# Two attention layers on one core: q and k kept in float32 in row tiles of 32, with the other TensorE jobs placed between the maxima

## The reference, cut to what matters

```python
q = split_heads(x @ Wq + bq)      # 16 heads of 16; x here is the layer-normalised x
k = split_heads(x @ Wk + bk)
v = split_heads(x @ Wv + bv)
attn = einsum('bhqd,bhkd->bhqk', q, k) / sqrt(16)
attn = attn + slopes[:, None, None] * (arange(T) - (T - 1))    # layer 0 only
attn = where(causal, attn, finfo.min)
o = einsum('bhqk,bhkd->bhqd', softmax(attn), v)
x = x + o @ Wo + bo
x = x + ffn(layernorm(x))         # layer 0: int weights, hidden 704; layer 1: fp8 weights, hidden 768
```

## Time and profile before

| | us |
|---|---|
| median of 3 runs | 438.63 |
| lowest, highest | 436.79, 441.16 |
| profiled execution, span | 441.7 |
| TensorE busy | 410.0 |
| VectorE busy | 297.1 |
| ScalarE busy | 232.9 |
| GpSimd busy | 170.2 |

### The profile page before, as it was taken

How to read it: one execution, slowest core, us unless ns; L and a number is a source line. 1 busy time by engine, 2 the same in 40 slices (tenths; PEclk the granted TensorE clock), 3 DMA queues, 4 the chain that set the end, 5 groups by cost and what they waited for, 6 DMA issues and landing times.

```text
span 441.7 us, 14528 instructions
## 1 busy us (share of the span) xinstructions
PE 410.0 (93%) x6328; PEld 237.2 (54%) x6328; DVE 297.1 (67%) x596; ACT 232.9 (53%) x377; POOL 170.2 (39%) x250
## 2 busy tenths in 40 slices
PE   5799789999999988999999998998999999888997
PEld 5356564555555347544377466544555553465476
DVE  4636489999998216521336586899999981188883
ACT  3535355577776973221101541655877769635950
POOL 4107013314033144478692000234361544453770
PEclk9989799999999999999999997999999999999999
DMA  6899550000000000200100479400000000000002
GB/s 204 129 239 263 128 148 4 4 3 4 4 2 5 4 1 6 65 8 9 64 0 0 120 200 224 106 5 4 3 4 3 4 5 2 2 1 0 1 26 71
DMA packets 21657, 22.97 MB, mean 52 GB/s; under 512 B 2588, under 2 KB 20858, under 8 KB 21594
## 3 DMA queue, kind: packets, MB, share of 16 engines
q1 hardware_dynamic: 20498, 19.03, 17.8%
q0 software_dynamic: 544, 2.49, 1.9%
q10 hardware_dynamic: 552, 0.53, 0.4%
HBM read 8.27 MB, written 1.05 MB: 21 GB/s over the span
## 4 chain that ended last, share of the span: by engine, by line
PE 71%; DVE 14%; ACT 4%; DMA 3%; issue 3%; POOL 2%; SPq 2%; ACTq 0%; DVEq 0%
PE ps L785 11%; PE ps L765 11%; DVE mx L1258 11%; PE ps L743 10%; PE ps L916 8%; PE ps L1012 5%; PE ps L944 4%; PE ps L921 4%; ACT prob L1141 4%; PE ps L677 4%; PE ps L980 4%; DMA col_rows<-in_L_ffn_up_scale 3%; PE ps L845 3%; PE ps L751 2%; POOL xn L605 1%
## 5 line engine op out<-in xcount | busy, mean ns | idle before, releaser
L1258 DVE TENSOR_REDUCE mx<-ps 128x1 f32<-128x512 f32 (+3 forms) x304 | 181.1, 654 | 28.9 <-PE ps L751 24.1
L1141 ACT ACTIVATE prob<-ps 128x1024 f32<-128x1024 f32 (+1 forms) x192 | 145.4, 812 | 63.4 <-PE ps L765 63.1
L743 PE MATMUL ps<-kS,qS 96*32 96x512 bf16 (+21 forms) x1536 | 111.9, 321 | 4.4 <-DVE mx L1258 3.0
L590 POOL TENSOR_SCALAR_AFFINE_SELECT prob<-prob 128x256 f32<-128x256 f32 x128 | 51.9, 412 | 163.9 <-ACT prob L1141 162.5
L765 PE MATMUL ps<-qS,kS 101*32 101x512 bf16 (+7 forms) x1536 | 95.2, 326 | 3.7 <-ACT prob L1141 3.6
L785 PE MATMUL ps<-prob,v 128*32 128x512 f32 (+3 forms) x768 | 80.1, 489 | 0.6 <-POOL prob L590 0.4
L743 PEld LDWEIGHTS ps<-kS,qS 99*32 99x32 bf16 (+1 forms) x1536 | 42.8, 95 | 50.4 <-DVE mx L1258 28.1
L748 PE MATMUL ps<-mask_q,identb 128*32 128x32 bf16 (+1 forms) x1024 | 51.1, 186 | 2.7 <-issue 2.7
L765 PEld LDWEIGHTS ps<-qS,kS 101*32 101x32 bf16 (+1 forms) x1536 | 35.0, 96 | 31.2 <-ACT prob L1141 15.8
L751 PE MATMUL ps<-mask_q,identb 128*32 128x64 bf16 (+1 forms) x512 | 45.4, 198 | 0.0
L748 PEld LDWEIGHTS ps<-mask_q,identb 128*32 128x32 bf16 x1024 | 28.1, 98 | 14.0 <-issue 9.2
(11 more groups left out here) (146 smaller groups left out, 537.0 us busy)
## 6 DMA issues: line engine op xcount, KB each, us to landing
qS<-parts SPq DMA_DIRECT2D x24, 128.0 KB, 3.3
kS<-parts SPq DMA_DIRECT2D x24, 128.0 KB, 3.4
qS<-prob SPq DMA_DIRECT2D x12, 128.0 KB, 8.0
kS<-prob SPq DMA_DIRECT2D x12, 128.0 KB, 7.5
qS<-xn SPq DMA_DIRECT2D x12, 128.0 KB, 3.4
kS<-xn SPq DMA_DIRECT2D x12, 128.0 KB, 2.9
out<-x SPq DMA_DIRECT2D x8, 128.0 KB, 1.7
oT<-in_L_ffn_gate_w POOLq DMA_DIRECT2D x1, 768.0 KB, 4.8
```

The source lines that it names most:

```text
L590: nc.gpsimd.affine_select(out=square, in_=square, compare_op=ALU.is_ge, fill=0.0, base=0, pattern=[[0, 2], [1, P]], channel_multiplier=-1) ...
L743: mmi = nc.tensor.matmul(span[r:r + STRIP, 0:seen], qS[0:K_MAX[L], c, g * G + h, qt * P + r:qt * P + r + STRIP], kS[0:K_MAX[L], g * G + h, ...
L1141: nc.scalar.activation(prob[:, n % 3, 2 * pair:2 * pair + 2, off:CH], ps[:, 2 * (m % 2):2 * (m % 2) + 2, off:CH], ACT.Exp, scale=SCALE).th ...
L1258: ins = nc.vector.tensor_reduce(mx[:, slot, qt, heads[0]:heads[-1] + 1, part], src, AX_X, ALU.max)
```

## The change

q and k are no longer cut into parts. A projection's output rows are laid out so that a tile of 128 rows holds four heads, one in each 32 rows (16 dimensions, then rows for alibi and the negated maximum, the remainder zero); the weights are padded into that layout (`wP`), with 16 projection jobs a layer in place of 8. ScalarE writes q and VectorE writes k straight into `qS` and `kS` in float32. Scores of a head are float32 products over its own 17 or 18 rows, at the row tile where the head stands (`place`), in four column strips as before. Heads are visited in an order that alternates between a group's two row tiles. The mask's small products use the head's own row tile. The maxima are turned in float32 with no negation or split (-1 stands in the rows of k). The alibi row is worked out on chip. All side jobs (12 of the 16 projections, v, weight turns, turns of xn) are entries of the list between the maxima, most of them in the ring of three banks; ScalarE empties most of them in the same order. GpSimd scales the first feed-forward weights between its triangle cuts.

```diff
+def place(u, l):
+    return 2 * (u % 2) + l // 2, 2 * (u // 2) + l % 2
 def qk_job(n):
-    return n // 2 % CJ, n // (2 * CJ), n % 2
-N_QK = CJ * NC * 2
+    return n // (2 * SLOTS), n // 2 % SLOTS, n % 2
+N_QK = NC * SLOTS * 2
+QK_B = 4
+HEADS = (0, 2, 1, 3)
...
     for qt in reversed(range(TPC)):
         keys = P * (qt + 1)
-        per = CH // keys
-        items += [(qt, 1, tuple(range(h, h + per)), CH * c, keys) for h in range(0, G, per)]
+        if 2 * keys > CH:
+            items += [(qt, 1, (l,), CH * c, keys) for l in HEADS]
+        else:
+            items += [(qt, 1, (l, l + 1), CH * c, keys) for l in range(0, G, 2)]
...
+def side_jobs(L):
+    at = [(2, ("xnT",))] + [(4 + 2 * t, ("v", t)) for t in range(V_A)]
+    at += list(zip((13, 15, 18, 20, 25, 27, 30, 32, 50, 53, 56, 59), [("qk", n) for n in range(QK_B, N_QK)]))
+    at += [(38 + 3 * n, ("v", V_A + n)) for n in range(NT - V_A)]
+    if L == 0:
+        at += [(22, ("cols",)), (34, ("bias",))]
+        turns = [(w, k) for w in ("gateT", "upT", "downT") for k in range(HT // 2)]
+        at += [(64 + 3 * n, job) for n, job in enumerate(turns)]
+        at += [(96 + 6 * m, ("w1T", m)) for m in range(4)]
...
-        qS = sb("qS", [P, NC, NH, CH], BF16)
-        kS = sb("kS", [P, NH, T], BF16)
+        qk = sb("qk", [P, 2, SLOTS, T], F32)
...
-            def spread(L, k):
...
             def spread_max(L, cg):
-                g, c = CGS[cg]
-                sp.wait_ge(mT_done, L * N_CG + cg + 1)
-                sp.dma_start(qS[K_MAX[L]:K_EXP[L], c, g * G:(g + 1) * G, :], mT[:, cg % 2, :]).then_inc(m_stacked[cg % 2], 16)
+                u, c = CGS[cg]
+                tile, slot = place(u, 0)
+                sp.wait_ge(m_free, TURNED[L][cg])
+                sp.dma_start(qS[slice(STRIP * tile + K_MAX[L], STRIP * (tile + 1) + K_MAX[L] + 1, STRIP), c, slot:slot + 2],
+                             mT[:, cg % 2, :]).then_inc(m_stacked[cg % 2], 16)
...
             def cut_triangles(L):
                 for s in TRI:
                     g, c, kt, off, _ = step_span(s)
+                    if L == 0 and TRI_AT[s] >= SCALES_FROM:
+                        for _n in range(min(SCALES_EACH, 2 * HT + CJ - len(scaled))):
+                            scale_next()
...
+            def projection_qk(L, bank, n):
+                c, slot, w = qk_job(n)
+                pe.wait_ge(a_free, A_AT["xnT", L, (c + 1) * TPC - 1] + 1)
+                for j in range(CJ):
+                    mmi = nc.tensor.matmul(bank[:, :], wP[:, L, w, j, slot], xnT[:, j, tokens(c)], start=j == 0, stop=j == CJ - 1)
+                return mmi
...
-            def max_scores(L, n, cg, item):
+            def max_scores(L, bank, cg, item):
+                u, c = CGS[cg]
                 qt, part, heads, key0, keys = item
+                for i, l in enumerate(heads):
+                    tile, slot = place(u, l)
+                    rows, own = tile_rows(tile, K_MAX[L]), tile_rows(tile, STRIP)
                     span = bank[:, i * keys:(i + 1) * keys]
                     for r in range(0, P, STRIP):
-                        mmi = nc.tensor.matmul(span[r:r + STRIP, 0:seen], qS[0:K_MAX[L], c, g * G + h, qt * P + r:qt * P + r + STRIP],
-                                               kS[0:K_MAX[L], g * G + h, key0:key0 + seen], start=True, stop=part == 0)
+                        mmi = nc.tensor.matmul(span[r:r + STRIP, 0:seen], qS[rows, c, slot, qt * P + r:qt * P + r + STRIP],
+                                               kS[rows, slot, key0:key0 + seen], start=True, stop=True)
                     if part == 1:
                         for r in range(0, P, STRIP):
+                            mmi = nc.tensor.matmul(span[r:r + STRIP, keys - P + r:keys], identb[own, own], mask_m[own, own.start:own.start + P - r],
+                                                   start=False, stop=True, skip_group_check=True)
...
             def exp_scores(L, s, pair):
...
                 for i in range(2):
-                    h = g * G + 2 * pair + i
+                    l = 2 * i + pair
+                    tile, slot = place(u, l)
+                    rows, own = tile_rows(tile, K_EXP[L]), tile_rows(tile, STRIP)
...
-                        mmi = nc.tensor.matmul(bank[r:r + STRIP, off:CH], kS[0:K_EXP[L], h, kt * P + r:kt * P + r + STRIP],
-                                               qS[0:K_EXP[L], c, h, off:CH], start=True, stop=not masked)
+                        mmi = nc.tensor.matmul(bank[r:r + STRIP, off:CH], kS[rows, slot, kt * P + r:kt * P + r + STRIP],
+                                               qS[rows, c, slot, off:CH], start=True, stop=not masked)
...
-            def qk_parts(L):
...
+            def take_q(L, n, bank):
+                c, slot, _w = qk_job(n)
+                bias = bqk[:, 0, slot:slot + 1] if L == 0 else 0.0
+                nc.scalar.activation(qS[:, c, slot], bank, ACT.Identity, bias=bias).then_inc(q_made, 1)
```

More of the change, by code:

```diff
@@ L152, in ring_b_jobs @@
         jobs += [("down", L, t) for t in DOWN_ORDER[L]]
+        jobs += [("none", L, n) for n in range(-len(jobs) % 4)]
     return jobs
 A_AT = {job: n for n, job in enumerate(ring_a_jobs())}
-B_AT = {job: n for n, job in enumerate(ring_b_jobs())}
+B_JOBS = ring_b_jobs()
+B_AT = {job: n for n, job in enumerate(B_JOBS)}
+B_FULL = {job: sum(j[0] != "none" for j in B_JOBS[:n + 1]) for n, job in enumerate(B_JOBS)}
+B_FREE = {job: sum(j[0] not in ("qk", "none") for j in B_JOBS[:n + 1]) for n, job in enumerate(B_JOBS)}
+HEADS = (0, 2, 1, 3)
 def max_items(c):
@@ L201, in attention_order @@
             entries.append(("max", cg, it))
+            n_max += 1
+            entries += [("side", job) for job in sides.get(n_max, [])]
             if waiting and n == T_LAG:
@@ L264 @@
 STEPS = exp_steps()
-ORDER = attention_order()
-N_MAX = sum(e[0] in ("max", "turn") for e in ORDER)
+ORDER = [attention_order(L) for L in range(LAYERS)]
+M_RING = [[e for e in order if e[0] in ("max", "turn") or (e[0] == "side" and not side_in_a(e[1]))] for order in ORDER]
+M_BASE = (0, len(M_RING[0]))
+M_OWN = [[sum(e[0] != "side" for e in ring[:n + 1]) for n in range(len(ring))] for ring in M_RING]
+M_OWN = [M_OWN[0], [M_OWN[0][-1] + n for n in M_OWN[1]]]
+TURNED = [[M_OWN[L][M_RING[L].index(("turn", cg))] for cg in range(N_CG)] for L in range(LAYERS)]
+MAXED = [[max(M_OWN[L][n] for n, e in enumerate(M_RING[L]) if e[0] == "max" and e[1] == cg) for cg in range(N_CG)]
+         for L in range(LAYERS)]
+OTHER_SIDES = [e[1] for e in M_RING[0] if e[0] == "side" and e[1][0] in ("cols", "gateT", "upT", "downT", "w1T")]
 LAST_STEP = {cg: max(s for s, x in enumerate(STEPS) if x[0] == cg) for cg in range(N_CG)}
@@ L284, in alibi_tail @@
 def alibi_tail():
-    bf16 = mybir.dt.np(BF16)
     start = 2.0 ** -0.5
     slopes = np.array([start * start ** i for i in range(NH)], np.float32)
-    bias = slopes[:, None] * (np.arange(T, dtype=np.float32) - np.float32(T - 1))[None, :]
-    rest = bias.astype(np.float32) / np.float32(SCALE)
-    rows = []
-    for _ in range(3):
-        part = rest.astype(bf16)
-        rows.append(part)
-        rest = rest - part.astype(np.float32)
-    rows += [np.ones((NH, T), bf16)] * (MAX_ROWS + ALIBI_ROWS[0])
-    apart = np.zeros((len(rows), NH * NC, CH + TAIL_GAP), bf16)
-    apart[:, :, 0:CH] = np.stack(rows).reshape(len(rows), NH * NC, CH)
-    return apart
+    columns = np.zeros((P, N_HC), np.float32)
+    for h in range(NH):
+        tile, slot = place(h // G, h % G)
+        columns[STRIP * tile + HD, slot] = slopes[h] / np.float32(SCALE)
+    columns[HD::STRIP, HC_ONE] = 1.0
+    for L in range(LAYERS):
+        columns[K_MAX[L]::STRIP, HC_NEG[L]] = -1.0
+    return columns.view(mybir.dt.np(BF16))
 def two_layer_kernel(nc, a, out, tail):
@@ new lines, in attention @@
+                        nc.tensor.matmul(bank[0:G * TPC, 0:P], top, ident[:], start=True, stop=True).then_inc(m_full, 1)
+                        m_n += 1
+                    elif entry[0] == "side" and entry[1][0] == "xnT":
+                        ln_transposes("xnT", 2 * L, 1, L, take_a, a_full)
+                    elif entry[0] == "side" and side_in_a(entry[1]):
+                        side_job(L, entry[1], take_a(("v", L, entry[1][1]))).then_inc(a_full, 1)
+                    elif entry[0] == "side":
+                        side_job(L, entry[1], take_m(L, m_n)).then_inc(m_full, 1)
@@ L1090, in _ @@
+            act.wait_ge(w0_in[0], 16)
+            act.wait_ge(w0_zero, 1)
+            for j in range(CJ):
+                nc.scalar.copy(padded(wP[:, 0, 0, j]), heads_apart(w0[:, 0, j])).then_inc(w0_turned, 1)
             for L in range(LAYERS):
```

694 lines of the change are left out of this document (338 added, 356 removed).

## The result

The changed kernel takes 790.11 us (four runs, 770.76 to 833.31) against 439.37 for the kernel before, 1.80 times as long. The two fastest runs alone, 770.76 and 777.54, give the ratio 1.766 (interval 1.751 to 1.781), since the others are over 1.5% above the fastest. The forecast was 511 us with a range of 450 to 595. The sign was right, the size was not: 351 us more, where the sum had 72.5. Unlike the kernel before, its time moves by some per cent from run to run, and with the granted clock: 770.76 us at 0.749 of full speed, 777.54 at 0.740, 802.67 at 0.714, 833.31 at 0.683. The profiled execution is the third of these, 800.9 us long.

What follows compares the result with a forecast made beforehand. TensorE was taken as the bound. Terms 30 + 27.5 - 16 - 10 + 21 + 20 = +72.5 on the execution's 441.7 gave 514.2, or 511 us from the median of 438.6; range 450 to 595.

Steps and rivals of the forecast that it cites:

- partly low: TensorE's clock before the first exponentials, where it waits: 0.89 and 0.91 in the two layers.
- Score products: Float32 heads on row tiles: 0.215 us on four tiles, 99 of 288 heads on two; +30 us.
- Changes of tiling: TensorE changes tiling twice in each of 96 steps, about 0.11 us each: +21 us.
- Masks: Diagonal heads' small mask products fall from six to four, 0.075 to 0.035 us a head: -10 us.
- The ring: Three banks for maxima: the fourth waits for the first's bank, 0.5 us in each of 39 full steps: +20 us.
- Waits and cold clock: Before the first exponentials, removing the bf16 parts and their moves gives back idle and low-clock time: -16 us.
- Projections: 16 projection jobs a layer in place of 8, each 1.72 us on the full array, nothing hiding them: +27.5 us.
- only two row tiles ever overlap: Rival for score products: float32's second pass queues ahead of the next head, all heads at 0.43, 592 us; chance 0.13.
- steps of 4.5 us or more: Sign in the profile after: steps lasting this long would show that the two-tiles rival is right.

Runs made afterwards that it cites:

- The replays: Layer 0's attention order played on TensorE alone, 32 rows, no waits; without masks, v products and side jobs 109.8 us in the kernel's tiles.
- the maxima in pairs: 32-row kernel, side jobs right behind the v product, maxima let out in even numbers: 597.71 us; with VectorE reducing only 32 columns, 583.59 us.
- the 32-row kernel: Changed kernel with every score product over all 32 rows of its row tile, not 17 or 18: 598.16 us, 1.367 times the kernel before.
- the two kernels of series: Two kernels of only float32 products on TensorE, in series by tiles and rows: 0.252 us a head on four tiles, 0.858 at full height.

## Why the prediction failed

**The failed step: a clock taken as given.** The prediction has the clock "partly low" only where TensorE waited, and booked the low clock as something to be won. No term asked whether the new products keep the clock. They don't: 192 us, over twice the change that was forecast, and no rival had it. It couldn't be read off the rows of before, where every product but the small ones covers 96 rows or more and the clock is 1.00 in every busy stretch. What could have been done is a rival: each product now fills 17 of 128 rows, and no row shows that at full clock.

**Score products, the term that was mis-sized.** +30 over both layers for float32 on tiles. The replays give 109.8 us a layer without masks against 83.2 in the sum: 53 more for both layers. The mechanism was as told (tiles do overlap, up to four heads at once, with starts within 0.12 us, and 0.43 a head on two tiles at full clock); wrong was the price of four tiles (0.252, not 0.215, which makes 14 of the 53) and the assumption that where exponentials and maxima stand on different tiles they always fill four. That is the other 39. The reading of the order is that the kinds come in clumps, two or one of a kind, then the other, with diagonal heads of other widths between; the replays show the size, not that this is all of it.

**Changes of tiling.** +21 at 0.11 each. By themselves they are 0.10 (the earlier trace rows was read rightly: eight times 0.215 behind 260.11 would end at 261.83, but the first record holds 0.1 longer than the others, which gives the 261.93). The Trainium skill, "TensorEngine Tiling (Array Packing)", Key Properties, has a change of mode drain the array, and these 0.10 us agree. In the order of the kernel they come to 0.20, 17 more for both layers. That each also cuts off strips that ran beside others would explain it; no run separates this. Yet on bf16 tiles and changes together cost 2.3 against full height.

**Masks.** The sum has them at 0.035 a diagonal head, 4.5 a layer; the replay 8.3.

**The ring.** +20, "0.5 in each of the 39 full steps". The waits of layer 0 are 3 to 5 us in all, shorter reductions give 7 over both layers, or 14 with the maxima in pairs. The step assumed that scores come in at 0.215 a head. At 0.40 (109.8 over 276), every other head a maximum, one comes each 0.8 us, and VectorE's 0.68 is in time. (The forecast's own numbers also give 1.71 and 2.57, not 1.75 and 2.65.) A term for a second bottleneck was added to a first one that had been priced too low.

**Waits and cold clock.** -16, and -10 for masks: the kernel with full-height bf16 scores and half the contraction shows +9.5 where the two terms have -26. The first exponentials did come earlier, as forecast (45 to 50 us; 59.27 before):

```profile
L1204 ACT ACTIVATE prob<-ps x2: 1024/1024/1024, 45.1 to 46.8; 128x1024 f32<-128x1024 f32 x2
```

But the work that stood ahead of them stands behind them now. An earlier start of one stage isn't time won while TensorE is the bound. How the 9.5 divide into order, side jobs and ScalarE's share was not tried.

**Projections.** +27.5; measured 23.1. The only additive term that held, since its duration came from a row of the same product at the same clock.

**The balance at full clock.** The forecast's span is 514.2, the 32-row kernel's 596.7: 82.5 missing. Scores +53, changes +17, masks in tiles +8, waits and masks removed +35, ring some -15, projections -4 are 94; the masks stand in two of these, and a replay is not the kernel, so the balance closes to 12 us and no better. The rival "only two row tiles ever overlap" (592) comes out near 598, and the forecast's sign for it, steps of 4.5 us or more, shows too (4.8). It is wrong all the same, and its number is luck: four heads stream at once in the timeline above, and where two tiles are all there is, a layer takes 123.8 us, against 109.8 in the kernel's order.

## What to carry to other kernels

Before trading bf16 parts for float32 on row tiles, price a head at what the order lets stream, not at one over the number of tiles; a replay of the order on TensorE alone, with nothing to wait for, gives that number in one run. A product that uses few rows of the array can pull the granted clock down while TensorE is fully busy; where zero rows are there anyway, include them, as one edit of two lines gave 192 us here, though one execution of a kernel with 32 rows lost the clock even so. None of the versions run beats the kernel before: the nearest that leaves nothing out, with 32 rows and maxima in pairs, is at 1.36.

## What the hardware showed that was not expected

- TensorE's granted clock fell to 0.50 (1.2 GHz) with the engine 100% busy: float32 products over 17 rows on one tile or two, and over 32 rows on one. Ahead of each series it had run full-height products at full clock. It stayed at 1.00 (2.4 GHz) for 24 and 32 rows on two tiles, for 17 rows on three or four, and for 17 rows on two with v products between. The Trainium skill, "TensorE: Matmul & The Clock Gate", Part 1, has the clock follow how busy the engine is; by that no series here should have lost it, and the rows of the two kernels of series decide otherwise. What exact mixture tips it in the kernel, where it changes level several times in a layer and differs from run to run, stays open.
- A float32 head costs 1.71 us on one tile (half clock), 0.425 on two (32 rows), 0.287 on three, 0.252 on four. With bf16, 160 heads on four tiles of 17 rows took 16.7 us, 0.105 each, at a mean clock of 0.73; full-height bf16 took 0.216 a head at full clock. Full height stands above, four tiles below:

```profile
482.00:516.00 34.00, 34.00 (x630) 16.67 (x632) 0.00 (x0) 0.00 (x0) 1.00 0.01 2
543.00:559.50 16.50, 12.87 (x639) 9.49 (x628) 0.00 (x0) 0.00 (x0) 0.73 0.02 4
```

- The 544 small bf16 mask products of layer 0 behind float32 strips cost 8.3 us on TensorE alone in the kernel's own tiles, 0.015 each. Packed on four tiles with the kinds apart they cost 19.3, some 14 without the share of the clock, 0.026 each.
